# Self attention of a decoder block: the weighted sums of two steps issued together, totals in an earlier slot

## The chip, the cores and the metric

The kernel runs on one core of a Trainium2 chip. The metric is device time in microseconds for one execution. In the text slot (2,1) of a group means kt = 2, j = 1.

## The reference

Eight sequences of 512 tokens of 512 numbers pass through one decoder block, all in float32. What matters here is the first of its three parts, causal self attention with 16 heads of 32 numbers:

```python
q, k, v = (_heads(q), _heads(k), _heads(x))
scores = jnp.einsum('bhqd,bhkd->bhqk', q, k) * scale
scores = jnp.where(causal, scores, -jnp.inf)
y_ar = jnp.einsum('bhqk,bhkd->bhqd', jax.nn.softmax(scores, axis=-1), v)
e = v[:, :, 1:, :] - y_ar[:, :, :-1, :]
ma = jnp.einsum('bhqd,bhkd->bhqk', qa, ka)   # qa, ka: leaky relu of q, sigmoid of k2
y_ma = jnp.einsum('bhqk,bhkd->bhqd', ma, e)
```

The values v are the input itself. The output of the part is (y_ar + y_ma) projected, added to the input and normalised. Then come cross attention with a projection, and two gated experts.

## The kernel before

The program has three phases: self attention (to about 660 us), the memory attention that needs y_ar, and cross attention with projection and experts, whose first slots are laid into the end of the second phase. The change touches the first phase alone.

**Groups, steps, slots.** Self attention is cut into 32 groups (8 sequences by 4 groups of 4 heads, PER = 4). A group has 16 slots (kt, j): kt is one of TILES = 4 tiles of 128 keys, j one of the 4 heads. The four slots of one kt are a step. `SELF_SLOTS` runs over all slots, and each engine's function walks the same list, issues what belongs to a slot and waits on semaphores for the others. So the order on each engine is written out by hand, and an engine can run ahead of another only as far as its buffers let it.

**A slot on TensorE** (`self_tensor`). First the transposed scores of (kt, j) (L296, operands of 98 rows, where two rows carry the negated maximum as a high and a low part), into bank 2 or 3; it waits until ScalarE has taken the exponentials of two slots ago. Then `self_scores` (L338), the plain scores of a slot 24 later, from which VectorE takes the maxima; three banks (0, 1, 5), so it waits for the maximum of three slots ago. Then one chunk of a projection, if `PROJECTED` names one: three matmuls of 512 columns (L201 to L203, high and low parts), q in slots (2,0) to (3,0), k in (3,1) to (0,0) into bank 6, k2 in (0,1), (0,2), (0,3) and (1,1).

**Sums and totals.** `self_weighted` multiplies a step's exponentials (tile pt, three buffers, one per step in turn) with v; the four heads go to four strips of 32 partitions of bank 4:

```python
for j in range(PER):
    done = pe.matmul(sh.bank[4][rows_of(j), first:SEQ], s.v[g % 2][:, kt, rows_of(j)], pt[:, j, 0:SEQ - first],
                     start=(kt == 0), stop=(kt == TILES - 1), skip_group_check=True)
```

Its columns are 512, 384, 256 and 128 for kt = 0 to 3. In the profile it is L351, eight instructions a block, since a float32 matmul is two. It stands in slot (kt, 1), two steps behind: steps 0 and 1 in (2,1) and (3,1), steps 2 and 3 in (0,1) and (1,1) of the next group. The softmax's denominators come from GpSimd, which masks each step's diagonal tiles (L594) and adds the steps up into `added` (L608); in slot (1,0) of the next group TensorE multiplies `added` by ones (L316, the totals, 512 columns, again four strips) into bank 6.

**What follows the totals.** VectorE turns bank 6 into reciprocals, 128 columns a slot (L543, k = 0 to 3), each behind the slot's maximum (L530, over 128, 256, 384 or 512 columns in turn), and then multiplies with the sums, which ScalarE has copied to `y_raw` (L430): the product L550 gives `y_ar`. In slot (2,2) TensorE transposes the next group's 16 maxima (L326) into the same bank 6. Its wait is

```python
pe.wait_ge(s.dve_norm, NORM * g)     # NORM = TILES + 1: four reciprocals and the product
```

ScalarE (L446) and VectorE (L555) split them into two parts, and SP stores them (`store_shift`, slot (3,0)) as the two extra rows that L296 needs from slot (0,0) of the next group.

**ScalarE** takes one exponential a slot (L412) and the copies of the projections (L417, L425, L435, L454, L458). **SP** issues, in slot order, the stack of q and k parts (12 transfers, slot (1,1), after VectorE's L537 of slot (0,2)), v (slot (1,3), after step 3's sums), the memory operands, the shift rows and y_ar.

The last groups have no projections left, as these run two or three groups ahead, and the first rounds of the memory phase are laid between their slots (`ROUND_AT`).

Of the kernel before, what the change touches and what calls it, by code (L numbers as in the profile page):

```python
# [18 lines left out]
TILES = SEQ // P  # L19
GROUPS = DIM // P  # L20
PER = P // HEAD_DIM
NG = BATCH * GROUPS
# [20 lines left out]
def split_slot(n):  # L43

    return n // SLOTS, n // PER % TILES, n % PER


def rows_of(j):
    return slice(HEAD_DIM * j, HEAD_DIM * j + HEAD_DIM)
# [231 lines left out]
def self_tensor(pe, s, second, third, cw, sh):  # L281
    pe.wait_ge(sh.const, CONSTS)
    pe.wait_ge(s.pool_ones, 3)
    for n in SELF_SLOTS:
        g, kt, j = split_slot(n)
        if n in ROUND_AT:
            memory_round_tensor(pe, s, second, third, cw, sh, ROUND_AT[n])
        if 0 <= n < NS:
            first = kt * P
            q0 = min(first, SEQ - 256)  # L290
            kq, bank = s.kq[g % 3], sh.bank[2 + n % 2]
            if kt == 0 and j == 0:
                pe.wait_ge(s.shift_landed[g % 3], 32 * (g // 3 + 1))
            if n >= 2:
                pe.wait_ge(s.act_exp, n - 1)
            pe.matmul(bank[:, 0:SEQ - q0], kq[0:98, 1, j, first:first + P], kq[0:98, 0, j, q0:SEQ],  # L296
                      start=True, stop=True).then_inc(s.pe_st, 1)
        m = n + SELF_LEAD
        if 0 <= m < NS:
            self_scores(pe, s, sh, m)  # L300
        if j == 1 and 0 <= n // PER - 2 < NG * TILES:
            self_weighted(pe, s, sh, n // PER - 2)
        if (kt, j) in PROJECTED:
            on, i = PROJECTED[kt, j]
            if 0 <= g + on < NG:
                self_project(pe, s, sh, g + on, i)
        if kt == 1 and j == 0 and 0 <= g - 1 < NG:
            d = g - 1
            pe.wait_ge(s.pool_add, 3 * (d + 1))
            pe.wait_ge(s.act_copied, d + 1)  # L310
            pe.wait_ge(s.dve_k, min(d + 4, NG))
            if d + 4 > NG:
                pe.wait_ge(s.dve_sh, min(d + 2, NG))
                pe.wait_ge(s.dve_norm, NORM * d)
            for jj in range(PER):
                done = pe.matmul(sh.bank[6][rows_of(jj), :], sh.ones[:, :], s.added[:, jj, :],  # L316
                                 start=True, stop=True, skip_group_check=True)
            done.then_inc(s.pe_tot, 1)
        if kt == 2 and j == 2 and 0 <= g + 1 < NG:
            d, n16 = g + 1, PER * TILES  # L320
            pe.wait_ge(s.dve_max, n16 * (d + 1))
            if g >= 1:
                pe.wait_ge(s.dve_norm, NORM * g)
            else:
                pe.wait_ge(s.dve_k, g + 3)
            pe.transpose(sh.bank[6][0:n16, 0:P], s.negmax[d % 2][:, :], sh.ident[:, :]).then_inc(s.pe_sh, 1)  # L326
    arrive(pe, sh.self_done)
# [14 lines left out]
def self_weighted(pe, s, sh, step):  # L342
    g, kt = divmod(step, TILES)
    first, pt = kt * P, s.pt[step % 3]
    pe.wait_ge(s.pool_mask, step + 1)
    if kt == 0:
        pe.wait_ge(s.v_landed[g % 2], 16 * (g // 2 + 1))
        if g > 0:
            pe.wait_ge(s.act_raw, g)
# [3 lines that stand above are left out]
    done.then_inc(s.pe_pv, 1)  # L353
# [31 lines left out]
def self_scalar(act, s, second, third, sh):  # L385
    for c in range(GROUPS):
        act.wait_ge(s.raw_landed[c], 16)
        act.activation(s.xt_hi[0][:, c, :], s.raw[c][:, :], ACT.Copy).then_inc(s.act_xt, 1)
    for i in range(2 * GROUPS):
        self_weight_high(act, s, i)  # L390
    act.wait_ge(s.dve_bias, 2)
    for n in SELF_SLOTS:
        g, kt, j = split_slot(n)
        if g == -2 and kt == 0 and j == 2:
            for i in range(2 * GROUPS, 3 * GROUPS):
                self_weight_high(act, s, i)

            self_x_high(act, s, GROUPS)
        if n in ROUND_AT:
            memory_round_scalar(act, second, third, sh, ROUND_AT[n])  # L400
        if 0 <= n < NS:
            step = n // PER
            first = kt * P
            q0 = min(first, SEQ - 256)
            if j == 0 and step >= 3:
                before = step - 3
                act.wait_ge(s.pe_pv, before + 1)
                act.wait_ge(s.pool_add, 3 * (before // TILES) + max(before % TILES, 1))
                if before % TILES == 0:
                    act.wait_ge(s.act_copied, before // TILES + 1)  # L410
            act.wait_ge(s.pe_st, n + 1)
            act.activation(s.pt[step % 3][:, j, 0:SEQ - first], sh.bank[2 + n % 2][:, first - q0:SEQ - q0], ACT.Exp,  # L412
                           scale=SCALE_SELF).then_inc(s.act_exp, 1)
        if kt == 0 and j == 1 and 0 <= g + 2 < NG:
            d = g + 2
            act.wait_ge(s.pe_k, d + 1)
            act.activation(s.stage[d % 2][:, 2, :].bitcast(F32R), sh.bank[6][:, :], ACT.Identity,  # L417
                           bias=bias_column(s, K, d)).then_inc(s.act_k, 1)
        if kt == 1 and j == 2 and 0 <= g + 2 < NG:
            d = g + 2  # L420
            ka = s.memory[:, 1, 1:SEQ]
            act.wait_ge(s.pe_k2, d + 1)
            if d >= 1:
                act.wait_ge(s.memory_stored, 16 * d)
            act.activation(ka, sh.bank[7][:, 0:SEQ - 1], ACT.Tanh, bias=bias_column(s, K2, d), scale=KSCALE).then_inc(s.act_k2, 1)  # L425
        if kt == 1 and j == (3 if g < NG else 2) and 0 <= g - 1 < NG:
            act.wait_ge(s.pe_pv, TILES * g)
            if g >= 2:
                act.wait_ge(s.dve_norm, NORM * (g - 1))
            act.activation(s.y_raw[:, :], sh.bank[4][:, :], ACT.Copy).then_inc(s.act_raw, 1)  # L430
        if kt == 2 and j == 0 and 0 <= g + 2 < NG:
            d = g + 2
            ka = s.memory[:, 1, 1:SEQ]
            act.wait_ge(s.act_k2, 2 * d + 1)
            act.activation(ka, ka, ACT.Copy, bias=1.0).then_inc(s.act_k2, 1)  # L435
        if kt == 2 and j == 1 and 0 <= g < NG:
            act.wait_ge(s.pool_mask, TILES * g + 1)
            if g >= 1:
                act.wait_ge(s.pe_tot, g)
            act.activation(s.added[:, :, 0:P], s.pt[TILES * g % 3][:, :, 0:P], ACT.Copy).then_inc(s.act_copied, 1)  # L440
        if kt == 2 and j == 3 and 0 <= g + 1 < NG:
            d = g + 1
            act.wait_ge(s.pe_sh, d + 1)
            if d >= 1:
                act.wait_ge(s.shift_landed[(d - 1) % 3], 32 * ((d - 1) // 3 + 1))
            act.activation(s.shift[:, 0, :].bitcast(F32R), sh.bank[6][0:PER * TILES, 0:P],  # L446
                           ACT.Copy).then_inc(s.act_sh, 1)
        if kt == 3 and j == 1 and 0 <= g + 3 < NG:
            d = g + 3
            if d >= 2:  # L450
                for jj in range(PER):
                    act.wait_ge(s.kq_landed[(d - 2) % 3][jj], 48 * ((d - 2) // 3 + 1))
            act.wait_ge(s.pe_q, d + 1)
            act.activation(s.stage[d % 2][:, 0, :].bitcast(F32R), sh.bank[7][:, :], ACT.Identity,  # L454
                           bias=bias_column(s, Q, d)).then_inc(s.act_q, 1)
            if d >= 1:
                act.wait_ge(s.dve_q, 2 * d)
            act.activation(s.relu[:, :], sh.bank[7][:, :], ACT.Relu, bias=s.bias_relu[:, d % GROUPS:d % GROUPS + 1],  # L458
                           scale=-RELU).then_inc(s.act_q, 1)
        if kt == 3 and j == 3 and GROUPS < g + 7 < NG:  # L460
            self_x_high(act, s, g + 7)
    arrive(act, sh.self_done)
# [36 lines left out]
def self_vector(dve, s, second, third, cw, sh):  # L499
# [15 lines left out]
    for n in SELF_SLOTS:  # L515
        g, kt, j = split_slot(n)
# [16 lines left out]
        if kt == 0 and j == 2 and 0 <= g + 2 < NG:  # L533
# [2 lines left out]
            dve.wait_ge(s.act_k, d + 1)  # L536
            dve.scalar_tensor_tensor(out=st[:, 3, :].bitcast(F32R), in0=sh.bank[6][:, :], scalar=bias_column(s, K, d),  # L537
                                     in1=st[:, 2, :], op0=ALU.add, op1=ALU.subtract).then_inc(s.dve_k, 1)
        k = PER * kt + j - PER - 1
        if 0 <= k < TILES and 0 <= g - 1 < NG:  # L540
            sums = sh.bank[6][:, tile_of(k)]
            dve.wait_ge(s.pe_tot, g)
# [1749 lines left out]
```

## Time and profile before

| | |
|---|---|
| runs, median (lowest to highest) | 1796.49 us (1793.62 to 1799.4), 3 runs |
| the profiled execution | 1795.43 us |
| its span, first to last instruction | 1793.7 us |
| mean granted TensorE clock | 0.974 |
| TensorE matmuls busy | 1712.4 us (95%) |
| VectorE / ScalarE / GpSimd busy | 1266.6 / 979.6 / 1182.2 us |

The profile is one execution. The difference between the profiled execution's time and its span lies around the program. TensorE's busy time is that of pipelined matmuls whose ends are modelled, so a start-to-start spacing says more than a duration. "PEld" is the weight load, which runs beside the matmul ahead. A row's bracket tells how long the engine was idle before it and who released it; "issue" means that it waited for nothing the profile shows.

### The profile page before, as it was taken

The page shows a single profiled execution, that of the slowest core. Times are in us where ns is not written, and L with a number is a line of the kernel's source. Part 1 is how long each engine was busy: PE and PEld are TensorE (multiplying, and loading weights), DVE is VectorE, ACT ScalarE, POOL GpSimd, SP SyncE. Part 2 cuts the span into 40 slices and gives each one's busy share as a digit, 9 for nine tenths or more (in the row PEclk, how much of TensorE's full clock was granted, in tenths as well). Part 3 has the DMA queues.
Part 4 walks back from the last instruction along what each step waited for, and adds up shares of the span by engine and source line. Part 5 has one row for each costly group of instructions (what it writes and reads, how often), then busy time and mean ns, then how long its engine had stood idle before and what let it go on. Part 6 is the DMA issues. An engine that isn't in the chain of part 4 may idle for free.

```text
span 1793.7 us, 30853 instructions
## 1 busy us (share of the span) xinstructions
PE 1712.4 (95%) x10602; PEld 1116.0 (62%) x10602; DVE 1266.6 (71%) x2792; ACT 979.6 (55%) x1931; POOL 1182.2 (66%) x969
## 2 busy tenths in 40 slices
PE   5999999999999989999998999999999999999997
PEld 4666666666666547887863456566565656656556
DVE  5677777777777656777876776877678686777744
ACT  3555555555555532433446656656566665666554
POOL 2556556556555454645567977868788787879783
PEclk9999999999999969999998999999999999999999
DMA  6555555565455454585625543435344353543210
GB/s 200 142 150 164 143 152 162 142 160 165 136 155 143 120 175 151 166 245 167 203 71 154 142 113 84 137 94 153 88 114 113 86 139 89 153 100 93 71 36 24
DMA packets 167272, 237.29 MB, mean 132 GB/s; under 512 B 22086, under 2 KB 73286, under 8 KB 167116
## 3 DMA queue, kind: packets, MB, share of 16 engines
q1 hardware_dynamic: 167116, 235.31, 47.5%
q8 instruction: 86, 1.41, 0.3%
q14 instruction: 70, 0.57, 0.1%
HBM read 91.57 MB, written 41.94 MB: 74 GB/s over the span
## 4 chain that ended last, share of the span: by engine, by line
PE 77%; DVE 6%; issue 4%; DMA 4%; POOL 3%; ACT 3%; SPq 2%; POOLq 0%; ACTq 0%; DVEq 0%
PE bank L201 8%; PE bank L1609 8%; PE bank L202 7%; PE bank L203 7%; PE bank L1482 6%; PE bank L1421 6%; PE bank L1450 5%; PE bank L351 5%; PE bank L296 5%; PE bank L338 4%; PE bank L1496 2%; PE bank L316 2%; DVE cross_negmax L1431 2%; PE bank L899 1%; PE bank L873 1%
## 5 line engine op out<-in xcount | busy, mean ns | idle before, releaser
L1431 DVE TENSOR_REDUCE cross_negmax<-bank 128x1 f32<-128x512 f32 x512 | 338.8, 675 | 157.0 <-PE bank L1421 154.4
L1693 ACT ACTIVATE cpt<-bank 128x512 f32<-128x512 f32 x512 | 297.4, 596 | 145.2 <-PE bank L1450 142.0
L530 DVE CUSTOM_DVE_ANT_0 bank<-bank,future 128x128 f32<-128x128 f32 (+3 forms) x512 | 246.7, 488 | 174.3 <-PE bank L338 173.6
L412 ACT ACTIVATE pt<-bank 128x256 f32<-128x256 f32 (+3 forms) x512 | 224.5, 441 | 257.3 <-PE bank L296 256.3
L1924 POOL TENSOR_TENSOR cross_added<-cross_added,cpt 128x2048 f32<-128x2048 f32 x64 | 293.7, 4590 | 12.9 <-ACT cpt L1693 12.5
L594 POOL TENSOR_SCALAR_AFFINE_SELECT pt<-pt 128x512 f32<-128x512 f32 x128 | 81.6, 638 | 252.4 <-ACT pt L412 252.4
L1450 PE MATMUL bank<-cqk 98*128 98x512 f32 x512 | 228.7, 447 | 8.3 <-ACT cpt L1693 8.1
L1421 PE MATMUL bank<-cqk 96*128 96x512 f32 x512 | 213.8, 421 | 16.4 <-DVE cross_negmax L1431 13.5
L1924 POOL TENSOR_TENSOR cross_added<-cpt,cpt 128x2048 f32<-128x2048 f32 x32 | 146.7, 4585 | 84.5 <-ACT cpt L1693 84.5
L201 PE MATMUL bank<-xt_hi,w_hi 128*128 128x512 f32 x384 | 168.9, 440 | 16.9 <-DVE w_lo L488 13.9
L296 PE MATMUL bank<-qk 98*128 98x256 f32 (+2 forms) x512 | 181.5, 358 | 3.5 <-DMA qk<-self_shift 2.4
L338 PE MATMUL bank<-qk 96*128 96x256 f32 (+2 forms) x512 | 166.7, 330 | 4.7 <-DMA qk<-stage 4.5
L1450 PEld LDWEIGHTS bank<-cqk 98*128 98x128 f32 x512 | 98.3, 192 | 108.1 <-issue 56.1
L202 PE MATMUL bank<-xt_hi,w_lo 128*128 128x512 f32 x384 | 153.4, 400 | 0.0
L203 PE MATMUL bank<-xt_lo,w_hi 128*128 128x512 f32 x384 | 152.8, 398 | 0.0
L1764 DVE RECIPROCAL bank<-bank 128x128 f32<-128x128 f32 x128 | 121.7, 954 | 37.0 <-PE bank L1515 37.0
L296 PEld LDWEIGHTS bank<-qk 98*128 98x128 f32 x512 | 98.8, 195 | 70.7 <-ACT pt L412 42.7
L1482 PE MATMUL bank<-cpt,cv 128*32 128x512 f32 x1024 | 141.0, 623 | 0.0
L1421 PEld LDWEIGHTS bank<-cqk 96*128 96x128 f32 x512 | 97.8, 193 | 54.9 <-DVE cross_negmax L1431 31.3
L201 PEld LDWEIGHTS bank<-xt_hi,w_hi 128*128 128x128 f32 x384 | 73.6, 192 | 88.9 <-issue 73.9
L543 DVE RECIPROCAL bank<-bank 128x128 f32<-128x128 f32 x128 | 122.1, 958 | 8.8 <-PE bank L316 8.8
L608 POOL TENSOR_TENSOR self_added<-self_added,pt 128x1024 f32<-128x1024 f32 x64 | 117.6, 1837 | 5.3
(203 smaller groups left out, 3666.8 us busy)
## 6 DMA issues: line engine op xcount, KB each, us to landing
qk<-stage SPq DMA_DIRECT2D x384, 128.0 KB, 2.3
cqk<-cstage SPq DMA_DIRECT2D x384, 128.0 KB, 2.4
scratch_memory<-memory SPq DMA_DIRECT2D x32, 512.0 KB, 3.8
ma<-scratch_memory SPq DMA_DIRECT2D x32, 512.0 KB, 4.0
raw<-in_x_t SPq DMA_DIRECT2D x32, 256.0 KB, 2.7
v<-in_x SPq DMA_DIRECT2D x32, 256.0 KB, 3.3
scratch_y_ar<-y_ar SPq DMA_DIRECT2D x32, 256.0 KB, 2.2
my_ar<-scratch_y_ar SPq DMA_DIRECT2D x32, 256.0 KB, 4.6
```

The source lines that it names most:

```text
L201: pe.matmul(out, a[0], b[0], start=first, stop=False)
L202: pe.matmul(out, a[1], b[0], start=False, stop=False)
L203: return pe.matmul(out, a[0], b[1], start=False, stop=last)
L296: pe.matmul(bank[:, 0:SEQ - q0], kq[0:98, 1, j, first:first + P], kq[0:98, 0, j, q0:SEQ], start=True, stop=True).then_inc(s.pe_st, 1)
L338: pe.matmul(bank[:, 0:max(keys, 256)], kq[0:96, 0, j, tile_of(qt)], kq[0:96, 1, j, 0:max(keys, 256)], start=True, stop=True).then_inc(s.pe ...
L530: dve.tensor_tensor_reduce(out=scores, in0=scores, in1=sh.future[:, SEQ - P * (qt + 1):SEQ], scale=-1.0, scalar=-NEG, op0=ALU.add, op1=ALU ...
L1421: pe.matmul(max_bank(sh, m)[:, :], kq[0:96, 0, jm, tile_of(qt)], kq[0:96, 1, jm, :], start=True, stop=True).then_inc(s.pe_mx, 1)
L1431: dve.reduce_max(s.negmax[gm % 2][:, col:col + 1], max_bank(sh, m)[:, :], AX, negate=True).then_inc(s.dve_max, 1)
L1450: pe.matmul(sh.bank[2 + n % 2][:, :], kq[0:98, 1, j, tile_of(kt)], kq[0:98, 0, j, :], start=True, stop=True).then_inc(s.pe_st, 1)
L1482: done = pe.matmul(sh.bank[4][rows_of(j), :], s.v[g % 2][:, kt, rows_of(j)], s.pt[step % 3][:, j, :], start=(kt == 0), stop=(kt == TILES - ...
L1693: act.activation(s.pt[step % 3][:, j, :], sh.bank[2 + n % 2][:, :], ACT.Exp, scale=SCALE_CROSS).then_inc(s.act_exp, 1)
L1924: pool.tensor_tensor(s.added[:, :, :], old[:, :, :], s.pt[step % 3][:, :, :], ALU.add).then_inc(s.pool_add, 1)
```

## The change

The separate blocks of weighted sums go. Steps 0 and 1 of a group are issued one behind the other in slot (2,3) of the same group, steps 2 and 3 in slot (0,3) of the next one, with the totals right behind them, in (0,3) where they were in (1,0). ScalarE's copy of the sums moves from slot (1,3) ((1,2) behind the last group) to (1,0). VectorE's reciprocals move from (1,1) to (2,0) to (1,0) to (1,3), its product from (2,1) to (2,0). No instruction and no transfer is added or removed; no buffer changes. The title's cross attention has no line in the diff.

```diff
--- before.py
+++ after.py
@@ -298,14 +298,18 @@
         m = n + SELF_LEAD
         if 0 <= m < NS:
             self_scores(pe, s, sh, m)
-        if j == 1 and 0 <= n // PER - 2 < NG * TILES:
-            self_weighted(pe, s, sh, n // PER - 2)
+
+        if (kt, j) == (2, 3) and 0 <= g < NG:
+            self_weighted(pe, s, sh, TILES * g)
+            self_weighted(pe, s, sh, TILES * g + 1)
         if (kt, j) in PROJECTED:
             on, i = PROJECTED[kt, j]
             if 0 <= g + on < NG:
                 self_project(pe, s, sh, g + on, i)
-        if kt == 1 and j == 0 and 0 <= g - 1 < NG:
+        if kt == 0 and j == 3 and 0 <= g - 1 < NG:
             d = g - 1
+            self_weighted(pe, s, sh, TILES * g - 2)
+            self_weighted(pe, s, sh, TILES * g - 1)
             pe.wait_ge(s.pool_add, 3 * (d + 1))
             pe.wait_ge(s.act_copied, d + 1)
             pe.wait_ge(s.dve_k, min(d + 4, NG))
@@ -423,7 +427,7 @@
             if d >= 1:
                 act.wait_ge(s.memory_stored, 16 * d)
             act.activation(ka, sh.bank[7][:, 0:SEQ - 1], ACT.Tanh, bias=bias_column(s, K2, d), scale=KSCALE).then_inc(s.act_k2, 1)
-        if kt == 1 and j == (3 if g < NG else 2) and 0 <= g - 1 < NG:
+        if kt == 1 and j == 0 and 0 <= g - 1 < NG:
             act.wait_ge(s.pe_pv, TILES * g)
             if g >= 2:
                 act.wait_ge(s.dve_norm, NORM * (g - 1))
@@ -536,7 +540,7 @@
             dve.wait_ge(s.act_k, d + 1)
             dve.scalar_tensor_tensor(out=st[:, 3, :].bitcast(F32R), in0=sh.bank[6][:, :], scalar=bias_column(s, K, d),
                                      in1=st[:, 2, :], op0=ALU.add, op1=ALU.subtract).then_inc(s.dve_k, 1)
-        k = PER * kt + j - PER - 1
+        k = PER * kt + j - PER
         if 0 <= k < TILES and 0 <= g - 1 < NG:
             sums = sh.bank[6][:, tile_of(k)]
             dve.wait_ge(s.pe_tot, g)
```

## Rows read from the trace of the kernel before

**Rows 1.** Windows view, 60 to 660 us: window, length, busy us of each engine.

```profile
60.00:595.00 535.00, 532.27 (x3062) 350.74 (x3062) 387.57 (x1149) 309.56 (x698) 304.65 (x222) 1.00 0.56 151
595.00:660.00 65.00, 58.84 (x321) 31.50 (x323) 34.14 (x89) 28.94 (x71) 38.28 (x43) 0.71 0.47 146
```

**Rows 2.** Timeline of TensorE, 400 to 440 us: start, duration (us), line.

```profile
404.80 0.27 PE L326 MATMUL bank<-ident,self_negmax 128*16 128x128 f32 x1
...
415.48 0.28 PE L338 MATMUL bank<-qk 96*128 96x256 f32 x1
415.69 1.06 PE L316 MATMUL bank<-self_added,ones 128*32 128x512 f32 x8
416.68 0.44 PE L296 MATMUL bank<-qk 98*128 98x384 f32 x1
416.96 0.28 PE L338 MATMUL bank<-qk 96*128 96x256 f32 x1
417.17 0.43 PE L351 MATMUL bank<-pt,v 128*32 128x128 f32 x8
417.53 0.50 PE L201 MATMUL bank<-xt_hi,w_hi 128*128 128x512 f32 x1
417.87 0.39 PE L202 MATMUL bank<-xt_hi,w_lo 128*128 128x512 f32 x1
418.10 0.39 PE L203 MATMUL bank<-xt_lo,w_hi 128*128 128x512 f32 x1
...
423.80 0.27 PE L326 MATMUL bank<-ident,self_negmax 128*16 128x128 f32 x1
```

**Rows 3.** Timeline of TensorE, 657 to 661 us.

```profile
658.23 0.64 PE L351 MATMUL bank<-pt,v 128*32 128x256 f32 x8
658.69 1.04 PE L316 MATMUL bank<-self_added,ones 128*32 128x512 f32 x8
659.55 0.40 PE L351 MATMUL bank<-pt,v 128*32 128x128 f32 x8
```

**Rows 4.** Timeline of VectorE, 415.7 to 424 us.

```profile
415.80 0.30 DVE L530 CUSTOM_DVE_ANT_0 bank<-bank,future 128x128 f32<-128x128 f32 x1 [0.23 <-PE bank L338]
416.01 0.14 DVE L530 DVE_READ_ACCUMULATOR2_ANT self_negmax<- 128x1 f32 x1
...
418.88 0.57 DVE L530 CUSTOM_DVE_ANT_0 bank<-bank,future 128x384 f32<-128x384 f32 x1 [0.29 <-PE bank L338]
...
420.24 0.64 DVE L530 CUSTOM_DVE_ANT_0 bank<-bank,future 128x512 f32<-128x512 f32 x1
...
421.66 0.24 DVE L530 CUSTOM_DVE_ANT_0 bank<-bank,future 128x128 f32<-128x128 f32 x1
...
421.81 0.96 DVE L543 RECIPROCAL bank<-bank 128x128 f32<-128x128 f32 x1
422.68 0.37 DVE L530 CUSTOM_DVE_ANT_0 bank<-bank,future 128x256 f32<-128x256 f32 x1
...
422.97 0.69 DVE L550 TENSOR_TENSOR y_ar<-bank,self_y_raw 128x512 f32<-128x512 f32 x1
```

**Rows 5.** Timeline of all engines around 613 us: the product and the transpose.

```profile
613.13 0.69 DVE L550 TENSOR_TENSOR y_ar<-bank,self_y_raw 128x512 f32<-128x512 f32 x1
...
613.97 0.27 PE L326 MATMUL bank<-ident,self_negmax 128*16 128x128 f32 x1 [1.46 <-DVE y_ar L550]
```

**Rows 6.** Waits, 60 to 595 us: total us, times, longest.

```profile
PEld bank L326 <- issue: 7.7, 28, 0.3
...
PEld bank L296 <- DMA qk<-self_shift: 1.9, 6, 0.7
```

**Rows 7.** Timeline of TensorE, 619 to 631 us.

```profile
618.88 0.50 PE L296 MATMUL bank<-qk 98*128 98x512 f32 x1 [1.91 <-DMA qk<-self_shift]
...
623.05 1.94 PE L316 MATMUL bank<-self_added,ones 128*32 128x512 f32 x8
```

**Rows 8.** Windows view, 620 to 625 us; the number before the last two is the granted clock.

```profile
620.00:625.00 5.00, 5.00 (x23) 2.06 (x15) 2.01 (x8) 2.27 (x5) 1.35 (x4) 0.50 0.00 0
```

## The prediction

> **What bounds the kernel now.** I read the windows view first. From 60 to 595 us, the steady part of self attention, TensorE is busy 532.27 of 535 us at a granted clock of 1.00, which is the 2.4 GHz level [rows 1]. VectorE is busy 72% there (387.57 of 535), ScalarE and GpSimd under 60%. So TensorE's own sequence sets the period, and the next view is its timeline over one group. The transpose of the maxima (L326) starts at 404.80 and again at 423.80 [rows 2]: a group lasts 19.0 us, and the window holds 28 of them. Call the first score matmul behind the totals T (416.68) and the transpose X (423.80). T to X is 7.12 us, X to T is 416.68 - 404.80 = 11.88 us [rows 2].
>
> **What a block of sums costs.** The totals block (512 columns, four heads, eight matmuls) starts 0.21 us after the score matmul ahead of it, where that one's 256 columns need 0.12 (415.48 to 415.69, against 416.96 less the same), so 0.09 is entry. The next matmul starts 0.99 later (416.68). The first matmul behind a block also spaces 0.34 from its successor where its kind spaces 0.23 (417.53, 417.87, 418.10): 0.11 more [rows 2]. Together 1.19. The same three parts for the 128-column block are 0.09, 0.36 (417.17 to 417.53) and 0.11: 0.56. The difference is 0.63 for 384 columns, that is 0.21 for each 128. So a block is 0.21 per 128 columns and 0.34 fixed: 1.19, 0.97, 0.77 and 0.56 for 512, 384, 256 and 128 columns. The blocks are cheaper in company: at 658 us, in the tail, where no other matmul lies between them, a 256-column block, the totals and a 128-column block start 0.46 and 0.86 apart [rows 3], which is streaming alone (0.43 and 0.85). I take the fixed 0.34 as paid once per run of neighbouring blocks.
>
> **The change on TensorE.** Before, a group has five separate blocks: steps 0 and 1 in slots (2,1) and (3,1), steps 2 and 3 in (0,1) and (1,1) of the next group, totals in (1,0). After, it has two: steps 0 and 1 in (2,3), and steps 2, 3 and totals in (0,3). Three fixed parts go: 3 x 0.34 = 1.0 us a group. For this the trace has both bounds: nothing saved, if each block kept its 0.34, and 1.0; rows 3 are the same instructions in the same order, so I take 1.0.
> What those rows show is that the price lies at the edges of a run. The Trainium skill, TensorEngine Tiling (Array Packing), Key Properties, says that changing the tiling mode drains the engine, while changing the tile within it doesn't; rows 2 and 3 agree. By that rule alone the sum would be the full 1.0 us a group, which is the first rival below.
>
> **The change on VectorE, and why the gain doesn't arrive.** X may not start until VectorE has written the last of five normalising operations on bank 6 (four reciprocals L543, one product L550), and they can't start until the totals stand. They interleave with the maxima, one per slot. Both versions put one reciprocal in each of four slots; after the change these are (1,0) to (1,3), product in (2,0). Work out the chain from T in the new order, from [rows 4]: the score matmul starts T, the maximum's matmul 0.28 later, lasts 0.28 (416.96 in rows 2), VectorE starts 0.04 on; first maximum of 128 columns 0.21 from idle (415.80 to 416.01); reciprocal 0.87 (421.81 to 422.68); maximum of 256 plus reciprocal 0.29 + 0.87 = 1.16; of 384 plus reciprocal 1.36 (418.88 to 420.24); of 512 plus reciprocal 1.42 (420.24 to 421.66); maximum of 128, 0.15; product 0.69. Sum 0.28 + 0.28 + 0.04 + 0.21 + 0.87 + 1.16 + 1.36 + 1.42 + 0.15 + 0.69 = 6.46. Where X visibly waited for the product, it started at 613.97, 0.15 after 613.13 + 0.69 [rows 5]. So T to X can't be under 6.61 us.
> TensorE's own work in T to X after the change: 7.12 less the 128-column block (0.56) and the 512-column one (1.19), plus the pair of slot (1,0), now behind the totals (0.18 + 0.12): 5.67. It will stand 0.9 us before X in every group. Before, it doesn't: the 28 idle spells ahead of X's weight load are put down to issue, 7.7 us in all, none to VectorE [rows 6], though the margin was thin, as the product ended at 422.97 + 0.69 = 423.66 and X followed at 423.80 [rows 2, 4]. The slower VectorE chain was hidden under blocks that now move out of this stretch.
> X to T: 11.88, less the blocks of 384 and 256 (0.97, 0.77), the old totals (1.19) and the pair of (1,0) (0.30); plus two runs of 0.34 + 0.85 + 0.64 = 1.83 and 0.34 + 0.43 + 0.21 + 0.85 = 1.83: 12.31. New period 12.31 + 6.61 = 18.92 against 19.00: **0.08 us a group**, where 1.0 was taken out.
>
> **Where other waits go.** ScalarE's copy of the sums (L430) moves from (1,3) to (1,0). It needs the sums of step 3, which are issued one slot before, and delays the exponential behind it by its own length; TensorE may then wait at (1,3), but it has the 0.9 us to lose before X, so this costs nothing; without that cover it would be a few tenths a group. GpSimd's addition of step 3 belongs to the slots (3,x), three slots ahead of the totals even now, and the wait for the split keys (L537, slot (0,2)) has a projection and the two blocks of sums ahead of it; what either were late would be added to the period one for one. The third pt buffer: exponentials of step 3 wait for the sums of step 0, now in the slot just ahead, but those stand before the score matmul in the same queue. On SP's queue no transfer is added; the load of v waits for step 3's sums and goes out behind the 12 stack loads as before. The shift rows reach st (0,0) with more room, as 1.83 us of sums now stand between X and it where 0.97 did: the 1.9 us of waits for that transfer [rows 6], some 1 us of the span after what they overlap, go.
> **Ends.** Ahead of the first X one 512-column block falls out and none comes in: -1.2. In the last three groups projections run out, TensorE waits for the shift transfer (1.91 us at 618.88 [rows 7]) and works at half clock, 0.50, which is 1.2 GHz [rows 8], where a 512-column block takes 1.94 [rows 7]. There a separate block used to be partly hidden in a wait; the run of two behind X at half clock is about 3.5 us, some 1.6 longer than one, under a wait of some 1 us of which part is left, and each run of three adds 0.3 behind the other wait. Less 0.5 for the shorter T to X, I take +1.2; bounds -1 and +4.
> **Sum**: 28 x -0.08 = -2.2, -1.0, -1.2, +1.2: **-3.2 us**. The profiled execution took 1795.43 (span 1793.7), so 1792.2; the median of the three runs is 1.06 above it, and I give 1793.0, between the two bases. The 0.08 is a difference of large numbers, read to 0.1: 28 x 0.1 = 3 us either way.
>
> **Rivals.**
> *The edges decide, not the chain*: 28 x -1.0 - 1.2 gives 1766. For it, rows 3; against it, the chain of 6.61, whose every term is a measured spacing, and VectorE can't start it before T. The Trainium skill's same page, Performance Considerations, warns that tiling speeds TensorE up but not the emptying of PSUM; that is the VectorE chain here, and rows 4 agree with it. A smaller form, X following the product at 0.05, gives 0.18 a group, 1790.
> *The clock (slower)*: the granted clock fell to 0.50 at 620 [rows 8] after stretches with waits of 1.5 to 2 us. The change puts 0.9 us of waiting before each X. If the fall comes one group earlier, or in a few groups, some 17 us of TensorE's work in that group takes up to twice as long: with half of it exposed, +8, 1801; it decides from the point where the 0.9 becomes 2. Against: 86% of T to X stays busy.
> *The merging saves nothing* (the change doesn't do what it says): each run keeps its fixed parts, 28 x (1.0 - 0.08) = +26, 1819. Against: rows 3.
>
> **Numbers.** Chain as worked out 0.73 (its own range 1787 to 1799, so it reaches a little past both bounds of no change); edges decide, in full or small form, 0.10; clock 0.12; merging void 0.05. A measurement of this kernel tells 0.3%, 5.4 us, from no change. Faster by over that (under 1791): 0.10 and some 0.17 of the first case: 0.27. Slower: 0.12 and 0.05, less the mild end of the clock case: 0.15. Range 1784 to 1801.
>
> **What would show it.** Right: T to X about 6.6 us, some 0.9 us idle ahead of X put down to y_ar L550, about 28 times; X to T 12.3; eight matmuls of 512 and eight of 384 columns, and eight each of 256, 128 and 512, without a gap; clock 1.00 to 595. Wrong: X without idle and a period near 18, a granted clock under 1 before 595, or gaps inside the merged runs.

## The result, and the profile after

| | before | after |
|---|---|---|
| median of 20 runs (lowest to highest) | 1794.85 us (1791.13 to 1803.62) | 1789.24 us (1785.15 to 1798.85) |
| profiled execution / its span | 1795.43 / 1793.7 us | 1788.97 / 1787.2 us |
| ratio, 95% interval | | 0.9971 (0.9960 to 0.9983) |
| instructions | 30853 | 30853 |

By the ratio the change is worth 5.2 us of 1795, 0.29% (the medians differ by 5.6): at the border of the 0.3%, 5.4 us, that the forecast called no change, and its interval lies wholly below 1, so there is a gain. The forecast was -3.2 us, a median of 1793.0. Lines move by four in the changed kernel: the transpose X is L330, the maxima L534, the reciprocals L547, the product L554, the sums L355, the totals L320.

First the windows view, answering to [rows 1] (busy us of TensorE, its weight load, VectorE, ScalarE, GpSimd; granted clock, DMA share, GB/s):

```profile
60.00:595.00 535.00, 517.15 (x3091) 354.16 (x3090) 382.54 (x1158) 305.11 (x705) 306.75 (x224) 1.00 0.56 153
595.00:660.00 65.00, 53.91 (x426) 30.62 (x428) 39.31 (x92) 29.78 (x73) 37.66 (x45) 0.84 0.46 140
```

TensorE is busy 15 us less in the same 535 us (532.27 before), at the same clock of 1.00. That is time taken out of its work and nearly none of it out of the kernel: it now waits. The timeline of TensorE over one period, answering to [rows 2], shows where:

```profile
401.18 0.27 PE L330 MATMUL bank<-ident,self_negmax 128*16 128x128 f32 x1 [0.52 <-DVE y_ar L554]
...
401.74 1.71 PE L355 MATMUL bank<-pt,v 128*32 128x512 f32 x16
403.38 0.38 PE L296 MATMUL bank<-qk 98*128 98x256 f32 x1
...
411.90 0.86 PE L355 MATMUL bank<-pt,v 128*32 128x256 f32 x16
412.57 1.04 PE L320 MATMUL bank<-self_added,ones 128*32 128x512 f32 x8
413.54 0.44 PE L296 MATMUL bank<-qk 98*128 98x384 f32 x1
413.82 0.28 PE L342 MATMUL bank<-qk 96*128 96x256 f32 x1
...
419.17 0.40 PE L203 MATMUL bank<-xt_lo,w_hi 128*128 128x512 f32 x1
420.08 0.27 PE L330 MATMUL bank<-ident,self_negmax 128*16 128x128 f32 x1 [0.52 <-DVE y_ar L554]
```

The pair of blocks takes 403.38 - 401.74 = 1.64 us and the run of three 413.54 - 411.90 = 1.64, which is streaming (1.49) plus one exit; the entry and the wider spacing behind stand outside. X to T is 413.54 - 401.18 = 12.36, T to X 420.08 - 413.54 = 6.54, the period 18.90. Ahead of X, TensorE's last projection starts at 419.17 and would let go at 419.40; X starts 0.68 later, and the bracket names the product. The chain on VectorE, answering to [rows 4]:

```profile
414.14 0.30 DVE L534 CUSTOM_DVE_ANT_0 bank<-bank,future 128x128 f32<-128x128 f32 x1 [2.09 <-PE bank L342]
...
414.35 0.96 DVE L547 RECIPROCAL bank<-bank 128x128 f32<-128x128 f32 x1
415.22 0.37 DVE L534 CUSTOM_DVE_ANT_0 bank<-bank,future 128x256 f32<-128x256 f32 x1
...
415.51 0.96 DVE L547 RECIPROCAL bank<-bank 128x128 f32<-128x128 f32 x1
416.38 0.51 DVE L534 CUSTOM_DVE_ANT_0 bank<-bank,future 128x384 f32<-128x384 f32 x1
...
416.80 0.96 DVE L547 RECIPROCAL bank<-bank 128x128 f32<-128x128 f32 x1
417.67 0.64 DVE L534 CUSTOM_DVE_ANT_0 bank<-bank,future 128x512 f32<-128x512 f32 x1
...
419.24 0.69 DVE L554 TENSOR_TENSOR y_ar<-bank,self_y_raw 128x512 f32<-128x512 f32 x1
```

From 414.14 to the product's end at 419.93 VectorE has no gap over ten operations (five maxima, four reciprocals, the product; a maximum's accumulator read begins together with the next operation), and before it 2.09 us of idleness: it stands still while TensorE makes the run of three, then TensorE stands still for it. X follows the product by 0.15. The waits of 60 to 595 us, answering to [rows 6], say the same 28 times:

```profile
PEld bank L330 <- DVE self_negmax L534: 25.9, 28, 0.9
PE bank L330 <- DVE y_ar L554: 14.5, 28, 0.5
PEld bank L296 <- ACT pt L416: 10.7, 28, 0.4
PEld bank L342 <- DVE self_negmax L534: 6.5, 28, 0.2
```

The weight load of X is held 0.9 us each time (put down to an instruction of VectorE's same stretch), and the wait for the shift transfer has gone from the list.

**Where the 6.5 us of span come from.** The 29 transposes from the first to the last of the steady part stand at 61.67 to 594.96 before and 60.98 to 590.18 after:

```profile
594.96 0.27 PE L326 MATMUL bank<-ident,self_negmax 128*16 128x128 f32 x1
```

```profile
60.98 0.27 PE L330 MATMUL bank<-ident,self_negmax 128*16 128x128 f32 x1
...
590.18 0.27 PE L330 MATMUL bank<-ident,self_negmax 128*16 128x128 f32 x1 [0.52 <-DVE y_ar L554]
```

0.7 us lie ahead of the first, 4.1 in the 28 periods (3.1 from 19.01 against 18.90, 1.0 from irregular periods such as 19.32 and 19.50 that no longer occur), and 1.5 between the last and the first projection of the memory phase; the rest of the program gives 0.2. That projection starts here, before and then after:

```profile
696.95 0.48 PE L201 MATMUL bank<-wproj_hi,y_hi 128*128 128x512 f32 x1
```

```profile
690.67 0.48 PE L201 MATMUL bank<-wproj_hi,y_hi 128*128 128x512 f32 x1
```

Only what the periods give repeats from profile to profile: the 28 sum to 533.3, 533.2 and 534.1 us in the three profiles with the old order in them (before, the fifth and the last experiment), and to 529.2, 529.0 and 529.4 in the three with the new one (after, after again, new to group 27). The stretches at either end differ between profiles of one order as well, as the last experiments show, and from the first projection of the memory phase to the end of the span, where no line changes, the ten profiles took 1095.4 to 1102.3 us. That the parts add up to 6.5 in this pair is no proof of the 1.5 and the 0.2.

### The profile page after: what moved, and what is told of

Read it like the earlier page. It is cut to its first block, busy times and chain, and to the rows that moved or that the text cites. A ratio compares the mean times of both kernels' runs of the same rounds, so it can differ in the third digit from the quotient of the medians.

```text
span 1787.2 us, 30853 instructions
## 1 busy us (share of the span) xinstructions
PE 1684.2 (94%) x10602; PEld 1113.5 (62%) x10602; DVE 1257.9 (70%) x2792; ACT 972.0 (54%) x1931; POOL 1180.6 (66%) x969
## 4 chain that ended last, share of the span: by engine, by line
PE 70%; DVE 15%; issue 4%; POOL 4%; DMA 3%; ACT 2%; SPq 1%; POOLq 0%; DVEq 0%; ACTq 0%
PE bank L1613 8%; PE bank L1486 6%; DVE bank L547 5%; PE bank L1425 5%; PE bank L1454 5%; PE bank L201 5%; PE bank L202 5%; PE bank L203 5%; PE bank L355 5%; PE bank L296 4%; PE bank L342 3%; DVE bank L534 2%; POOL cross_added L1928 2%; PE bank L1500 2%; DVE cross_negmax L1435 2%
## 5 line engine op out<-in xcount | busy, mean ns | idle before, releaser
L534 DVE CUSTOM_DVE_ANT_0 bank<-bank,future 128x128 f32<-128x128 f32 (+3 forms) x512 | 243.0, 489 | 175.8 <-PE bank L342 175.7
L416 ACT ACTIVATE pt<-bank 128x256 f32<-128x256 f32 (+3 forms) x512 | 217.9, 445 | 260.1 <-PE bank L296 258.3
L296 PE MATMUL bank<-qk 98*128 98x256 f32 (+2 forms) x512 | 179.4, 356 | 5.6 <-ACT pt L416 3.6
L342 PE MATMUL bank<-qk 96*128 96x256 f32 (+2 forms) x512 | 169.8, 335 | 4.9 <-DMA qk<-stage 4.0
L201 PE MATMUL bank<-xt_hi,w_hi 128*128 128x512 f32 x384 | 157.5, 410 | 15.9 <-DVE w_lo L492 13.9
L296 PEld LDWEIGHTS bank<-qk 98*128 98x128 f32 x512 | 97.0, 191 | 85.1 <-issue 49.2
L547 DVE RECIPROCAL bank<-bank 128x128 f32<-128x128 f32 x128 | 122.5, 960 | 10.3 <-PE bank L320 10.3
L342 PEld LDWEIGHTS bank<-qk 96*128 96x128 f32 x512 | 97.7, 191 | 25.4 <-DVE self_negmax L534 7.6
```

The source lines that it names most:

```text
L201: pe.matmul(out, a[0], b[0], start=first, stop=False)
L342: pe.matmul(bank[:, 0:max(keys, 256)], kq[0:96, 0, j, tile_of(qt)], kq[0:96, 1, j, 0:max(keys, 256)], start=True, stop=True).then_inc(s.pe ...
L534: dve.tensor_tensor_reduce(out=scores, in0=scores, in1=sh.future[:, SEQ - P * (qt + 1):SEQ], scale=-1.0, scalar=-NEG, op0=ALU.add, op1=ALU ...
```

## The experiments

Two theories stood against each other. The chain: since the change, VectorE's ten operations (the expectations say nine) between totals and transpose set the period, so whatever shortens them or puts TensorE's work beside them brings the full saving. The edges: only the number of separate runs of sums counts, and VectorE's part is incidental. The medians below are set against the kernel before on the same chip (1796.3 us for the first four, 1794.58 for the others). The diffs of the first four are against the changed kernel.

**Shorter reciprocals.** This kernel leaves out the inversion of three quarters of the totals, so its output is not the reference's.

```diff
-            dve.reciprocal(sums, sums)
+            sums = sh.bank[6][:, P * k:P * k + 32]
+            dve.reciprocal(sums, sums)
```

> The changed kernel, with each of the four reciprocals of a group over 32 columns where it was over 128; the other 96 columns keep the bare totals, so the product is left wrong there. Nothing moves on TensorE. Theory (VectorE's nine operations between totals and transpose set the period): they get some 2 us shorter, TensorE's own work decides, period 12.36 + 5.7 = 18.05 us against 18.90, so 28 x -0.85 = -24 us against the changed kernel, about 1766, and no wait of the transpose for y_ar. Rival (the merged runs starve ScalarE or save only a part of the edges, VectorE is innocent): period 18.6 or more, under 8 us gained.

1768.27 us, ratio 0.9841 (0.9807 to 0.9876). Not one instruction of TensorE was touched. Its timeline:

```profile
255.98 0.44 PE L296 MATMUL bank<-qk 98*128 98x384 f32 x1
...
261.63 0.27 PE L330 MATMUL bank<-ident,self_negmax 128*16 128x128 f32 x1
...
279.43 0.40 PE L203 MATMUL bank<-xt_lo,w_hi 128*128 128x512 f32 x1
279.67 0.27 PE L330 MATMUL bank<-ident,self_negmax 128*16 128x128 f32 x1
```

T to X is 5.65 us (5.67 in the prediction's working), X follows the projection by 0.24 with no wait, and the period is 18.04; a few periods of 19.0 to 19.6 among the 28 come from shift rows that are now late (from 60 to 560 us the score matmuls' weight loads wait 6.8 us for them in all, the matmuls 3.9). The reciprocals' mean fell from 961 to 361 ns, and the kernel from the changed one's 0.9971 to 0.9841. So the merging does save its full 0.9 to 1.0 us a group, and VectorE held it back.

**The pairs without the earlier totals**: one part of the change alone.

```diff
         if (kt, j) == (2, 3) and 0 <= g < NG:
             self_weighted(pe, s, sh, TILES * g)
             self_weighted(pe, s, sh, TILES * g + 1)
+        if (kt, j) == (0, 3) and 0 <= g - 1 < NG:
+            self_weighted(pe, s, sh, TILES * g - 2)
+            self_weighted(pe, s, sh, TILES * g - 1)
...
-        if kt == 0 and j == 3 and 0 <= g - 1 < NG:
+        if kt == 1 and j == 0 and 0 <= g - 1 < NG:
             d = g - 1
-            self_weighted(pe, s, sh, TILES * g - 2)
-            self_weighted(pe, s, sh, TILES * g - 1)
...
-        if kt == 1 and j == 0 and 0 <= g - 1 < NG:
+        if kt == 1 and j == (3 if g < NG else 2) and 0 <= g - 1 < NG:
...
-        k = PER * kt + j - PER
+        k = PER * kt + j - PER - 1
```

> The pairs of weighted sums as in the change, but totals, ScalarE's copy, reciprocals and product in their old slots. Theory: edges 2 x 0.34 are saved, but TensorE's work from totals to transpose is 5.4 us and VectorE's chain behind totals in (1,0) stays 6.6 to 6.7, while totals to transpose begins one slot later: X to T 11.88 - 0.97 - 0.77 + 1.83 + 0.98 = 12.95, period 19.6 to 19.7, so 28 x 0.6 = +17 us against the kernel before, about 1812. Rival (edges alone decide): 19.01 - 0.68 = 18.33, -19 us, about 1776.

1810.64 us, ratio 1.008 (1.0057 to 1.0104): slower than the kernel before, though two edges a group fewer. TensorE's timeline:

```profile
287.59 1.07 PE L320 MATMUL bank<-self_added,ones 128*32 128x512 f32 x8
288.58 0.44 PE L296 MATMUL bank<-qk 98*128 98x384 f32 x1
...
295.25 0.27 PE L330 MATMUL bank<-ident,self_negmax 128*16 128x128 f32 x1 [1.17 <-DVE y_ar L554]
...
314.89 0.27 PE L330 MATMUL bank<-ident,self_negmax 128*16 128x128 f32 x1 [1.11 <-DVE y_ar L554]
```

T to X 6.67, period 19.64. TensorE's own work there is 1.3 us shorter than VectorE's chain (7.12 - 0.56 - 1.19 = 5.37), and the sums moved out of it (1.75) come back in X to T less the two edges (0.68): 12.96 against 11.89. The edges alone would have given about 1776; this is the run that rules that theory out.

**The transpose behind the pair.** Nothing is left out.

```diff
-        if kt == 2 and j == 2 and 0 <= g + 1 < NG:
+        if kt == 2 and j == 3 and 0 <= g + 1 < NG:
             d, n16 = g + 1, PER * TILES
```

> The changed kernel with the transpose one slot later, in (2,3), behind the two blocks of sums: 1.8 us of TensorE's work now lie under VectorE's chain. Nothing is left out. Theory: no wait of the transpose for y_ar, period 18.05 to 18.2, -20 to -24 us against the changed kernel, about 1767; ScalarE and VectorE split the maxima later, still before the k projection in (3,1). Rival (the split and its transfer are then late, so the wait moves to the k projection or to slot (0,0)): period 18.7 to 19.

1768.64 us, ratio 0.9840 (0.9803 to 0.9878), the best kernel of this study whose output is complete:

```profile
271.15 0.45 PE L296 MATMUL bank<-qk 98*128 98x384 f32 x1
...
277.49 1.71 PE L355 MATMUL bank<-pt,v 128*32 128x512 f32 x16
279.13 0.28 PE L330 MATMUL bank<-ident,self_negmax 128*16 128x128 f32 x1
...
297.28 0.28 PE L330 MATMUL bank<-ident,self_negmax 128*16 128x128 f32 x1
```

The transpose starts where the pair ends, with no bracket, and the period is 18.15. Its waits from 60 to 560 us:

```profile
ACT self_shift L450 <- PE bank L330: 48.3, 28, 1.7
...
PEld bank L296 <- DMA qk<-self_shift: 2.9, 7, 1.1
```

ScalarE now stands 1.7 us before the split of each group's maxima, which costs nothing, as its next exponential needs a matmul behind the same transpose. The transfer of the shift rows is late at times (periods of 18.3 to 19.1 among those of 18.15), which is the rival's wait in a small form.

**Step 0's sums ahead of the transpose.**

```diff
-        if (kt, j) == (2, 3) and 0 <= g < NG:
-            self_weighted(pe, s, sh, TILES * g)
+        if (kt, j) == (2, 1) and 0 <= g < NG:
+            self_weighted(pe, s, sh, TILES * g)
+        if (kt, j) == (2, 3) and 0 <= g < NG:
             self_weighted(pe, s, sh, TILES * g + 1)
```

> The changed kernel with the sums of step 0 alone in slot (2,1), ahead of the transpose, step 1 in (2,3): one edge more (0.34 us), but 1.19 us of work under VectorE's chain. Theory: TensorE 5.7 + 1.2 = 6.9 from totals to transpose against VectorE's 6.54, so no wait; X to T 12.36 - 0.85 = 11.5; period 18.35 to 18.4, -15 us against the changed kernel, about 1774. Rival (edges decide): +0.34 a group, +9.5 us, about 1799.

1778.1 us, ratio 0.9891 (0.9857 to 0.9925):

```profile
275.45 0.45 PE L296 MATMUL bank<-qk 98*128 98x384 f32 x1
...
279.53 1.06 PE L356 MATMUL bank<-pt,v 128*32 128x512 f32 x8
...
282.32 0.27 PE L331 MATMUL bank<-ident,self_negmax 128*16 128x128 f32 x1
...
300.75 0.27 PE L331 MATMUL bank<-ident,self_negmax 128*16 128x128 f32 x1
```

T to X 6.87, no wait, periods of 18.37 (this one, at 18.43, is one of the longer). With one edge more than the changed kernel it is some 14 us faster ((0.9971 - 0.9891) x 1796): undoing one of the two merged runs wins, because the block now lies beside VectorE's chain.

**The transpose later in the kernel before.** The same one-line edit as above, made there.

> The kernel before, with the transpose one slot later, in (2,3), and nothing else. Theory: before, TensorE reaches the transpose just as the product is ready, so there is nothing to win: period 19.0, 0 to -1.5 us (the small irregular waits for the shift rows could grow or shrink). Rival (moving the transpose is worth something by itself): period under 18.8.

1790.71 us, ratio 0.9973 (0.9956 to 0.9991). The period is 18.98, as the theory has it, so the edit gives 0.03 us a group there and 0.75 in the changed kernel. The 4 us of the median are more than the 0 to 1.5 expected and more than that explains (28 x 0.03 = 0.8; with the irregular ones the 28 periods take 533.2 us against 533.3). The interval reaches down to 1.6 us. Part of the rest goes with the clock: the mean granted clock was 0.978 in these ten runs and 0.976 in the 34 of the kernel before, and among those 34 a clock higher by 0.001 goes with a time shorter by 1.1 us, which makes some 2.5 us. Whether the edit raises the clock or the runs happened to have it is open.

**The changed kernel again, and its two halves in time.** A function of the group chooses the order, in the kernel before; for the first half it is

```diff
+def new(d):
+    return d < 28
...
-        if kt == 1 and j == 0 and 0 <= g - 1 < NG:
+        if (kt, j) == ((0, 3) if new(g - 1) else (1, 0)) and 0 <= g - 1 < NG:
             d = g - 1
+            if new(d):
+                self_weighted(pe, s, sh, TILES * g - 2)
+                self_weighted(pe, s, sh, TILES * g - 1)
```

and likewise for the sums, ScalarE's copy and the reciprocals; for the second half it is d >= 28.

> The changed kernel once more, on the chip of the next two: about -5.6 us against the kernel before, which fixes the scale for them.

> The new order for groups 0 to 27, the old one for the sums, totals, copy and reciprocals of groups 28 to 31. Theory (the steady part is 28 x -0.11 plus irregular waits that go, the rest of the gain lies in the last groups): -4.5 to -5 us against the kernel before. Rival (the last groups lose 1.2, as forecast): as good as the changed kernel or 1 us better, -6 to -7.

> The new order for the groups from 28 on alone. Theory: -1.5 us. Rival (as forecast): +1.2 us.

Measured: 1789.75 us, 0.9966 (0.9946 to 0.9985); 1789.88 us, 0.9965 (0.9948 to 0.9982); 1795.36 us, 0.9998 (0.9977 to 1.0018). With the new order in groups 0 to 27 alone the kernel is as fast as the changed one, so what the change brings lies there. The last groups give 0, with an interval of some 4 us either way, which holds both -1.5 and +1.2: their share is not settled, and neither run tells its theory from its rival. The windows view shows one reason why single profiles can't settle it. These are the longest stretches at the lower clock in the last groups: before, after, and in the kernel with the new order to group 27:

```profile
620.10:657.50 37.40, 34.88 (x165) 16.97 (x158) 14.29 (x29) 15.67 (x39) 22.11 (x26) 0.50 0.46 149
```

```profile
623.60:637.00 13.40, 11.10 (x51) 4.28 (x52) 1.74 (x4) 3.64 (x10) 8.79 (x13) 0.50 0.55 190
```

```profile
626.80:636.80 10.00, 9.49 (x41) 2.98 (x41) 1.20 (x3) 3.88 (x10) 6.09 (x10) 0.50 0.68 233
```

The first and the third run the same order of the last groups, and one stays at 1.2 GHz for 37.4 us at a stretch, the other for 10. From 595 to 660 the mean granted clock was 0.71 before and 0.84 after, and 0.89 in the kernel of the fifth experiment, whose code there is almost that of before. The two ends of self attention, in the six profiles that bear on them (us; "last" is from the last steady transpose to the first projection of the memory phase):

| profile | first groups | last groups | first transpose to second | last |
|---|---|---|---|---|
| before | old | old | 16.24 | 101.99 |
| before, transpose later | old | old | 16.16 | 97.79 |
| new from group 28 | old | new | 16.01 | 100.69 |
| after | new | new | 15.05 | 100.49 |
| after, again | new | new | 14.71 | 99.46 |
| new to group 27 | new | old | 15.44 | 98.24 |

The first column of times is shorter wherever the first groups have the new order; the last column doesn't sort by order. (In the kernel with the later transpose it starts some 0.3 us later in its period.)

## Why the prediction was right, point by point

- **What bounds, before**: held. The period was TensorE's 19.0 us, and moving the transpose in that kernel changed it by 0.03.
- **The price of a block, 0.34 fixed, paid once per run**: held. The changed kernel's TensorE work is 18.04 us a group once VectorE is out of the way, against 17.98 worked out (12.31 + 5.67), and X to T with pairs alone was 12.96 against 12.95.
- **The chain, T to X not under 6.61**: the mechanism held 28 times in 28; the size was 6.54. The one term that differs is the maximum of 384 columns with its reciprocal, taken as 1.36 from a row in which the maximum began after an idle spell; straight behind a reciprocal it took 417.67 - 416.38 = 1.29. X to T was 12.36 where 12.31 was worked out, so the errors cancelled in part: 18.90 against 18.92, 0.11 us a group where 0.08 was said.
- **The wait ahead of X, 0.9 us**: held (the weight load is held 0.9). On the matmul itself 0.68 is visible, since 0.2 was already lost on the way, in the wait of L342 for a maximum and of L296 for the exponential behind ScalarE's copy; the working named the second of these.
- **Other waits**: no wait of TensorE for GpSimd, for the pt buffers or for SP's queue is in the list from 60 to 595 us, apart from 0.5 us in all for the stack of q and k parts (0.3 before). The irregular waits for the shift rows went, 1.0 us as was said.
- **Ends**: The start was right. The block falls out between the first two transposes, and that gap was 16.24 and 16.01 us with the old order against 15.05, 14.71 and 15.44 with the new one: about 1.1 less, where 1.2 was said. The first of the steady transposes came only 0.7 us sooner in this pair of profiles, as where the very first one starts differs by up to 2.2 us (43.76 to 45.93). The last groups were forecast at +1.2, and no run confirms it: the pair of profiles gave -1.5, with the one before at half clock for 37.4 us at a stretch, and the timed halves 0 within 4 us. The sum without it would have been -4.4, beside -5.2 measured; the 0.11 a group for 0.08 makes up the other 0.8. So -3.2 fell 2 us short by an unproved term for the last groups and by a steady gain taken too small.
- **The rivals**: the edges alone (1766) is what the kernel would have been without the chain: 1768.3 with short reciprocals and 1768.6 with the transpose moved. It failed for the reason given. The clock stayed at 1.00 to 595 us with 0.9 us of waiting in each group. The merging was not void.
- The Trainium skill's rule on switching modes (TensorEngine Tiling (Array Packing), Key Properties) agrees with the runs: the price lies at the edges of a run of blocks (a period of 18.04 against 17.98 worked out), though no run separates the change of tiling mode from what else changes at such an edge. By itself it would have misled by over 20 us. Its remark on emptying PSUM on the same page (Performance Considerations) named the side that decided, and the run with short reciprocals agrees with it.

## What to carry to other kernels

Work that is taken off the busiest engine pays only where nothing else was just fitting beside it: before moving a block, add up the other engines' chain across the stretch that it leaves. Here two engines took turns waiting (2.09 us and 0.9 us in each group), and the cure was to put the freed work beside the chain, not to take out more: the same edges, with one instruction placed behind the block instead of ahead of it, gave 1.6% where the change gave 0.3%. An undoing that looks backward, one edge more, can win for the same reason.

## What the runs showed that I had not expected

A maximum over 384 columns took 0.42 us to its accumulator read directly behind a reciprocal (416.38 to 416.80) and 0.48 when VectorE had been idle before it. The working took 0.49 from [rows 4] by difference; the rows of the kernel before show it:

```profile
418.88 0.57 DVE L530 CUSTOM_DVE_ANT_0 bank<-bank,future 128x384 f32<-128x384 f32 x1 [0.29 <-PE bank L338]
419.37 0.14 DVE L530 DVE_READ_ACCUMULATOR2_ANT self_negmax<- 128x1 f32 x1
```

The same 0.06 us stands at 128, 256 and 512 columns (0.15, 0.29 and 0.55 behind a reciprocal, 0.22, 0.35 and 0.62 from idle). It is the reciprocal ahead that makes the difference and not that VectorE was busy: behind the product, with no idle time between, the 384 columns took 0.47. So a chain's terms are best taken from rows with the same operation ahead.

And an idle spell of TensorE of almost 1 us in every 19 left the granted clock at 1.00 through 535 us, while in the stretch of the last groups the clock averaged 0.71, 0.84 and 0.89 over 65 us in three kernels that differ little there.
